# A gated two-layer block on one core: expert matmuls in FP32 without splits, sixteen feed-forward panels loaded during routing, eleven from the 37th expert block on

## The reference

```python
x = x + tanh(g_xattn[0]) * cross_attention(layernorm(x), ctx)       # 64 context rows per sequence
x = x + tanh(g_ffn[0])   * moe(layernorm(x))                        # see below
x = x + tanh(g_xattn[1]) * (layernorm(x) @ W1.T + mean(ctx) @ W2.T + b)
x = x + tanh(g_ffn[1])   * ternary_ffn(layernorm(x))                # 256 -> 1024 -> 1024 -> 1024 -> 256

def moe(x):   # 16 experts, hidden width 128, two experts per token
    scores = softmax(x @ gate_w); w, idx = top_k(scores, 2); w = w / sum(w)
    h = silu(x @ w1[e]) * (x @ w3[e]);  y = h @ w2[e]               # for both chosen experts e
    return sum(w * y) + x
```

## Time and profile before

| | |
|---|---|
| median of the runs | 514.05 us |
| runs | 511.73 to 516.06 us (3) |
| the profiled execution | 516.89 us, span 514.8 us |
| TensorE busy | 482.9 us (94%) |
| VectorE, ScalarE, Pool busy | 317.2, 214.0, 147.2 us |
| mean granted TensorE clock | 0.973 |
| moved by transfers | 58.81 MB |

### The profile page before, as it was taken

How to read it: one execution, slowest core, us unless ns; L and a number is a source line. 1 busy time by engine, 2 the same in 40 slices (tenths; PEclk the granted TensorE clock), 3 DMA queues, 4 the chain that set the end, 5 groups by cost and what they waited for, 6 DMA issues and landing times.

```text
span 514.8 us, 7849 instructions
## 1 busy us (share of the span) xinstructions
PE 482.9 (94%) x2754; PEld 414.0 (80%) x2754; DVE 317.2 (62%) x850; ACT 214.0 (42%) x444; POOL 147.2 (29%) x154
## 2 busy tenths in 40 slices
PE   8898977994889899999999999999999999999996
PEld 7787867893879678888987888897888888788886
DVE  3988855872668577548456874537677633745433
ACT  4569924671547695621254221126222133621210
POOL 1677674647562141101071110126011101000000
PEclk9989997997799999999999999999999999999999
DMA  8967432795572558422041220005032002021101
GB/s 290 339 251 245 156 93 83 211 290 167 166 220 94 177 185 268 148 81 61 22 143 43 64 78 24 1 1 163 22 102 62 1 1 81 2 77 66 42 1 47
DMA packets 34480, 58.81 MB, mean 114 GB/s; under 512 B 4545, under 2 KB 18369, under 8 KB 34370
## 3 DMA queue, kind: packets, MB, share of 16 engines
q1 hardware_dynamic: 29776, 47.12, 27.9%
q0 software_dynamic: 3840, 10.49, 7.2%
q10 hardware_dynamic: 818, 0.61, 0.4%
HBM read 47.85 MB, written 14.42 MB: 121 GB/s over the span
## 4 chain that ended last, share of the span: by engine, by line
PE 77%; DVE 4%; another core or an unknown queue 3%; ACT 2%; issue 2%; DMA 1%; POOLq 0%
PE bank L2038 23%; PE bank L2039 23%; PE bank L2010 6%; PE bank L2007 5%; PE bank L1613 3%; PE bank L1615 3%; PE bank L1614 3%; PE bank L2071 3%; PE bank L2070 3%; PE bank L1850 2%; PE bank L1853 1%; DVE turned L1019 1%; ACT xb L1429 1%; DMA xg_more<-xb_dram,perm 1%
## 5 line engine op out<-in xcount | busy, mean ns | idle before, releaser
L1587 ACT ACTIVATE sg<-bank,colv 128x512 f32<-128x512 f32 x64 | 44.1, 690 | 177.2 <-PE bank L2039 177.2
L2038 PE MATMUL bank<-Ah,Wr 128*128 128x512 f32 x256 | 100.3, 392 | 0.6 <-DVE sg L1296 0.6
L2038 PE MATMUL bank<-Bh,Wr 128*128 128x512 f32 x256 | 99.9, 390 | 0.0
L2039 PE MATMUL bank<-Bl,Wr 128*128 128x512 f32 x256 | 99.7, 389 | 0.0
L2039 PE MATMUL bank<-Al,Wr 128*128 128x512 f32 x256 | 99.7, 389 | 0.0
L2038 PEld LDWEIGHTS bank<-Ah,Wr 128*128 128x128 f32 x256 | 48.0, 188 | 11.9 <-DVE sg L1296 1.4
L2039 PEld LDWEIGHTS bank<-Bl,Wr 128*128 128x128 f32 x256 | 48.1, 188 | 9.8
L2038 PEld LDWEIGHTS bank<-Bh,Wr 128*128 128x128 f32 x256 | 48.1, 188 | 9.8
L2039 PEld LDWEIGHTS bank<-Al,Wr 128*128 128x128 f32 x256 | 48.1, 188 | 9.7
L1313 DVE CAST Ah<-sg 128x512 fp32r<-128x512 f32 x32 | 13.6, 426 | 60.1 <-ACT sg L1587 60.1
L1613 PE MATMUL bank<-EL,turned 128*128 (+1 forms) x133 | 42.7, 321 | 1.2 <-issue 0.9
(11 more groups left out here) (295 smaller groups left out, 1036.9 us busy)
## 6 DMA issues: line engine op xcount, KB each, us to landing
Wraw<-panels SPq DMA_DIRECT2D x44, 256.0 KB
stage<-panels SPq DMA_DIRECT2D x44, 256.0 KB
ES<-experts SPq DMA_DIRECT2D x16, 384.0 KB, 5.7
ys_dram<-yb SPq DMA_DIRECT2D x47, 128.0 KB
ys_dram<-x SPq DMA_DIRECT2D x1, 1920.0 KB, 8.8
X<-x SPq DMA_DIRECT2D x3, 512.0 KB, 7.8
xb_dram<-xb SPq DMA_DIRECT2D x3, 512.0 KB, 4.5
out<-outb SPq DMA_DIRECT2D x3, 512.0 KB
```

The costliest lines, as they stand in the source:

```text
L1587: eng.activation(sg[:, (8 * layer + m) % 3, :], bank[m % 4][:, :], ACT.Gelu, scale=colv[:, c + m:c + m + 1]).then_inc(f_act[m], 1)
L2038: mm(bank[m % 4][:, :], Wr[:, base:base + P], h[0][:, k, :], start=k == 0, stop=False)
L2039: ins = mm(bank[m % 4][:, :], Wr[:, base:base + P], h[1][:, k, :], start=False, stop=k == FK - 1 and not general)
```

## The change

- The experts are no longer split. All sixteen are loaded unsplit to `EW` (FP32), with no wait, over `Ah`, `Al`, `Bh`. `split_high`, `split_low`, `expert_low` and the buffers `ES` go.
- Gate, up and down are one FP32 matmul each per 128 of depth: three per block for nine. `turned` is FP32, in four buffers, copied by ScalarE alone (`rows_turned`); `low` goes. The first `gate_up` waits for all experts.
- The top sixteen panels of `Wr` are now free during routing. A new function `home` puts panels 0 to 15 there; SP loads eight behind the first group's `store_rows` and eight behind the second's. Panels 16 to 26 are loaded at blocks 36 to 46, one each, and 27 to 43 when the loop is over (those from 38 on after the first layer).
- Fill transfers stand behind experts 7, 13 and 15; all `store_rows` behind the experts.
- Eight gather buffers for six, two product buffers for three, `down` three blocks later instead of four, the permutation after block 1 instead of 2, the comparisons for it (`block_hot`) ahead of the loop. The y gathers go two at a time at blocks 32 to 35; the written-out numbers of the first group's steps move by about one.

```diff
-PAN_AT = 8
-
-FILL_AT = (10, 11)
-DVE_LOW_AT = (5, 7, 9, 11)
-
-PERM_AT = 2
-FIRST_PAN = NRAW + (3 * 4 * 4 * 256) // (4 * 512)
+PAN_AT, PAN_BETWEEN = 36, 11
+
+FILL_FIRST, FILL_AT = 7, (13, 15)
+
+PERM_AT = 1
+FIRST_PAN = 2 * NRAW + (3 * 4 * 4 * 256) // (4 * 512)
...
-Y_AT = (28, 29, 31, 32, 34, 35, 37, 38)
-ROOT2_AT, ROW_AT, ROOT3_AT = (37, 45), (38, 45), (44, 46)
-ADD_AT, STAT_AT = (25, 28, 31, 36), (26, 29, 33, 37)
-TURN3_AT, HIGH3_AT, LOW3_AT, PART_AT, X3_AT = (30, 37), (31, 38), (32, 39), (33, 40), (34, 41)
+Y_AT = (32, 32, 33, 33, 34, 34, 35, 35)
+ROOT2_AT, ROW_AT, ROOT3_AT = (38, 45), (39, 45), (44, 46)
+ADD_AT, STAT_AT = (27, 29, 32, 35), (28, 30, 33, 36)
+TURN3_AT, HIGH3_AT, LOW3_AT, PART_AT, X3_AT = (31, 38), (32, 39), (33, 40), (34, 41), (35, 42)
 NORM_AT, TURN4_AT, HIGH4_AT, LOW4_AT = (43, 45), (44, 47), (45, 48), (46, 48)
...
-NXG = 6
-DOWN = 4
+NXG = 8
+DOWN = 3
...
-        put = over(e_off, b_end)
-        EH, EL = put("EH", [P, E * EXP_COLS], F32R), put("EL", [P, E * EXP_COLS], F32R)
+        put = over(w_end, bl_off)
+        EW = put("EW", [P, E * EXP_COLS])
+        put = over(bl_off, b_end)
+        XT = 4
+        turned = [put(f"turned{b}", [P, JW]) for b in range(XT)]
+        xg_late = put("xg_late", [P, NXG - 6, D])
...
+        def home(w):
+
+            return (w + NPAN - NRAW) % NPAN * PANEL
...
-            eng.dma_start(Wraw[:, w * PANEL:(w + 1) * PANEL], panels[w]).then_inc(dma_pan[w % 4], 16)
+            eng.dma_start(Wraw[:, home(w):home(w) + PANEL], panels[w]).then_inc(dma_pan[w % 4], 16)
...
             def load_expert(e):
-                if e >= NES:
-
-                    eng.wait_ge(pool_el, EL_CUT * (e - NES + 1))
-                eng.dma_start(ES[:, e % NES, :], experts[e]).then_inc(dma_exp[e % NES], 16)
+                eng.dma_start(EW[:, e * EXP_COLS:(e + 1) * EXP_COLS], experts[e]).then_inc(dma_exp[e % 2], 16)
...
-            for e in range(NES, E):
+            for e in range(E):
                 load_expert(e)
-                if e == NES + 1:
+                if e == FILL_FIRST:
 
                     eng.dma_start(ys_dram[T * TOPK:NBLK * P, :], x[0:NBLK * P - T * TOPK, :]).then_inc(dma_fill, 16)
                 if e in FILL_AT:
                     n = T * TOPK - E * P
                     a, b = (n * (FILL_AT.index(e) + k) // len(FILL_AT) for k in range(2))
                     eng.dma_start(ys_dram[E * P + a:E * P + b, :], x[a:b, :]).then_inc(dma_fill, 16)
-                if e == 12:
-                    store_rows(0, 0, TG)
-            store_rows(1, 0, TG)
-
-            store_rows(2, 0, TG)
+            for g in range(NG - 1):
+                store_rows(g, 0, TG)
+                if g < 2:
+                    for w in range(NRAW // 2 * g, NRAW // 2 * (g + 1)):
+                        load_raw(eng, w)
             eng.wait_ge(dve_xb, 2)
             eng.dma_start(xb_tiles[:, NT - 2:NT, :], xb[:, 1, 2:TG, :]).then_inc(dma_xb[1], 16)
             store_rows(NG - 1, 0, 2)
...
-            panel_at = [PAN_AT + 3 * (w // 2) + w % 2 if w < DVE_PAN else PAN_AT + 12 + 2 * (w - DVE_PAN) for w in range(NRAW)]
+            panel_at = [PAN_AT + n for n in range(PAN_BETWEEN)]
...
-            split_low(2)
-            factor1(1)
-            split_low(2)
-            eng.wait_ge(dve_pn, 1)
-            factor1(2)
-            split_low(2)
-            factor1(3)
-            split_low(2)
+            for g in range(1, NG):
+                factor1(g)
             for g in range(NG):
-                if g > 0:
-                    eng.wait_ge(dve_ohr, g)
-                    split_low(2)
-                if g < NG - 1:
-                    eng.wait_ge(dve_pn, g + 2)
-                else:
-                    eng.wait_ge(dve_both, NG)
-                split_low(3 if g < NG - 1 else 1)
                 factors2(g)
...
-                if i in Y_AT:
-                    gather_rows(0, [Y_AT.index(i)])
+                gather_rows(0, [n for n in range(TOPK * TG) if Y_AT[n] == i])
...
-                if i < 2:
-                    block_hot(i)
-                if i <= PERM_AT:
+                if i < NBLK:
                     product(i)
-                    if i == PERM_AT:
-                        experts_of_blocks()
-                        eng.wait_ge(pe_perm, 2)
-                        permuted(bank_y[0], slice(E, NBLK))
-                    low(i + 2)
-                else:
-                    low(i + 2)
-                    if i < NBLK:
-                        product(i)
-
+                if i == PERM_AT:
+                    experts_of_blocks()
+                    eng.wait_ge(pe_perm, 2)
+                    permuted(bank_y[0], slice(E, NBLK))
                 if i == PERM_AT + 1:
                     block_experts()
-                if i in DVE_LOW_AT:
...
-            def high_turned(n):
-                b, w = n % 3, joint(n)
+
+
+            def rows_turned(n):
                 eng.wait_ge(b_tx, n + 1)
-                eng.activation(turned_pair(n)[0][:, w], bank_t[b][:, w], ACT.Copy).then_inc(b_xh, 1)
+                eng.activation(turned[n % XT][:, joint(n)], bank_t[n % 3][:, joint(n)], ACT.Copy).then_inc(b_xt, 1)
...
             def gate_up(i, at_):
-                high_, low_ = turned_pair(i)
-                eng.wait_ge(b_xl, i + 1)
+                eng.wait_ge(b_xt, i + 1)
+                if i == 0:
+                    eng.wait_ge(dve_counts, 1)
+                    for b in range(2):
+                        eng.wait_ge(dma_exp[b], 16 * (E // 2))
                 if i >= 2:
 
                     eng.wait_ge(b_h, i - 1)
                 for k in range(DK):
-                    w = bass.ds(at_ + k * 2 * H, 2 * H)
-                    x_k = slice(k * P, (k + 1) * P)
-                    ins = three(bank_gu[i % 2][:, 0:2 * H], (high_[:, x_k], low_[:, x_k]), (EH[:, w], EL[:, w]),
-                                k == 0, k == DK - 1)
+                    ins = mm(bank_gu[i % 2][:, 0:2 * H], turned[i % XT][:, k * P:(k + 1) * P],
+                             EW[:, bass.ds(at_ + k * 2 * H, 2 * H)], start=k == 0, stop=k == DK - 1)
                 ins.then_inc(b_gu, 1)
 
             def down(i, at_):
-                eng.wait_ge(b_xl, i + 5)
+                eng.wait_ge(b_xt, i + 5)
                 if i == 0:
 
                     eng.wait_ge(dve_perm, 2)
                 elif i >= 2:
                     eng.wait_ge(b_ye, i - 1)
-                w = bass.ds(at_ + 2 * DK * H, D)
-                h = (i + 4) % 3
-                three(bank_y[i % 2][:, 0:D], (t_high[h][:, DK * P:JW], t_low[h][:, DK * P:JW]), (EH[:, w], EL[:, w]),
-                      True, True).then_inc(b_y, 1)
+                mm(bank_y[i % 2][:, 0:D], turned[i % XT][:, DK * P:JW], EW[:, bass.ds(at_ + 2 * DK * H, D)], start=True,
+                   stop=True).then_inc(b_y, 1)
 
 
             offsets = [e * EXP_COLS for e in range(E)]
```

## The result

The changed kernel took 517.73 us (median of six runs, 517.11 to 522.37) beside 512.2 us for the kernel before in the same runs: a ratio of 1.0112, with an interval of 1.0074 to 1.015. I had predicted 504.5 with a range of 496 to 514. It became slower by about 5.5 us where I expected it to become faster by 9.5.

A forecast was written before the change was run, and what follows sets the result against it. TensorE's matmul chain was taken to bound the block loop at 1.40 us a block, with 32 us of waits or lower clock besides. +10 - 18 - 0.5 - 2 + 1 = -9.5 us gave 504.5 for the median, range 496 to 514.

The forecast's parts named there:

- Matmuls in FP32: Expert blocks: three FP32 matmuls for nine FP32R make a block 1.62 us against 1.40, +10 us if TensorE stays the bound.
- The remainder: Block stage: the 32 us in which TensorE waited or ran at the lower level fall to 14, -18 us.
- Eight buffers and the new place of the sums' gathers: Block loop, sums' gathers at blocks 32 to 35: a TensorE wait of about 1 to 3 us replaces 15.
- Panels: Routing: sixteen panels moved there fit only just, last stores following at 61 to 62; +1 us (0 to +5).
- Splits: Routing: without Pool's expert splits, VectorE's small instructions beside them no longer stretch; -2 us (bounds 0 and -4).
- The stalls stay: Block stage, rival: stalls come with Pool's unbroken gather bursts, so about 32 us stay; +7.5, 521.5 us, chance 0.12.
- less than 5 of the 32 us go: Block stage: the point from which the slow rival, 521.5 us, was to be decided; its chance 0.12.

The follow-up runs named there:

- fp32r_nine: Changed kernel with nine FP32R matmuls per block again, on high parts, instead of three FP32: 514.29 us with stalls, 493.13 without.
- y_old: Changed kernel with the sums' gathers at the block numbers of before (28 to 38) instead of 32 to 35: 519.07 us, ratio 1.0106, with stalls.
- loop_panels: Changed kernel with its first sixteen panels loaded at blocks 4 to 19, one each, instead of in routing: 493.33 us, ratio 0.9948, without stalls.
- splits_back: `loop_panels` with 24 subtractions of Pool put back into routing where the expert splits were, on a scratch tile: 515.82 us, ratio 1.0059, with stalls.
- after_again: Changed kernel, unchanged, run and profiled again beside the kernel before: 518.55 us, ratio 1.0087, with stalls.

## Why the prediction was wrong, point by point

- **Matmuls in FP32.** The step was right: 1.62 us by six records, +10.3 in the floor. What followed, "+10 if TensorE stays the bound", was not what it was worth. Without stalls B stayed at 86.7 for 86.8, and by `fp32r_nine` the longer step is worth 3.5 to 4.3 us of time.
- **The remainder, 32 to 14, -18 us.** This is the step that failed. With stalls it went from 32.1 and 29.1 (two profiles of before) to 23.7 and 25.4, by about 6; without, from 14.5 to 4.1, by 10.4. I had put it down to rows that land late because Pool is behind. That mechanism exists, and the sets without stalls show it (5.3 us of waits for landings in B before, none after); but in the sets with stalls, from which the profile came, it was not the main one. There TensorE's results reached ScalarE late while Pool issued gathers without a pause, and the change left such rows of gathers in place. The sign was in the rows that I read: ScalarE waited 4.53 us for the result that it took at 130.14, and no wait of TensorE behind 119.72 named a landing. By the count of records that result was complete at 118.29, 11.9 us earlier. I charged the whole stall to the 1.08 us wait for a landing at 119.72.
- **Eight buffers and the new place of the sums' gathers.** The place is worth nothing with stalls (`y_old`). Whether the buffers or the longer step closed the 10.4 us without them was not taken apart beyond this: with nine FP32R matmuls and eight buffers the remainder is 83.2 - 72.3 = 10.9, so 3.6 of the 10.4 come without the longer step and the other 6.8 with it.
- **Panels, +1 us (0 to +5).** Wrong in size: F to T grew from 7.2 to 11.6, 13.8 and 12.3 us, so +4.4 to +6.6; `loop_panels` gives all of it back. I forecast the last landing at 61 to 62, and Pool's first gather came at 61.7, 62.7 and 64.2. I compared that with the 65.21 of a profile in which routing happened to end late, and did not ask what the earlier end of VectorE's chain would be worth if the stores did not follow it. The store's longer way (+2.9) and TensorE's lower clock after the wait (+1.4) are what my +1 left out.
- **Splits, -2 us in routing.** Too small, by profiles: the factors are ready at 54.5 to 54.8 in three of the changed kernel and at 57.20, 60.83 and 62.72 in three of before, so the gain is 2.6 to 8 us. The casts take 0.17 us four times, as forecast. Putting Pool's part back cost about 1 us, so most of the gain belongs to something else that the change did to routing (ScalarE's splits, the loads of the experts that no longer wait); this was not taken apart.
- **The sum** by measured terms, with stalls, all from the means of two profiles each: factors 54.5 for 59.0, -4.5; F to T 12.7 for 7.2, +5.5; B 107.1 for 102.9, +4.2; together +5.2. Measured: +5.5 and +4.6 (518.55 against 513.94). Without stalls there is one profile of each: F to T +5.1, B -0.1, and factors 54.75 for 62.72; but the profiled execution of before was 4.7 us above the median of its set, so the last term is worth less than the 8.0 that it shows. Measured: +1.1 (497.18 for 496.1).
- **The rivals.** "The stalls stay" named what happened: unbroken gathers, a remainder that hardly falls, a result slower than before, with +7.5 for the measured +5.5. I gave it 0.12. Its decisive point ("less than 5 of the 32 us go") was missed narrowly, at about 6. Against it I had written that TensorE waits for a landing at 119.72; that was the wrong row to weigh.

A version that beats both kernels without stalls is `loop_panels` (0.993 to 0.995). With stalls it was not run; `splits_back`, the same with Pool's work added, is at 1.0059 there, below the changed kernel's 1.0087 in the same set.

## What to carry to other kernels

When a consumer gets its data microseconds after the producer's last record and no landing is named, do not explain the gap by the nearest late transfer: replace the suspected neighbours by work of the same length that moves nothing. When a step frees an engine ahead of a store, look at what stands before that store on its queue, and at the clock of the engine that waits for it: here panels and rows ahead of the last store took back most of what routing had gained. And read a stage's length from more than one profile before counting microseconds in it: the last factors of the same kernel came at 57.2, 60.8 and 62.7.

## What was unexpected of the hardware

The same program lost 15 to 21 us of its block stage in stalls in some sets of runs and none in others (before: B of 101.4 and 104.4 against 86.8; changed: 106.3 and 108.0 against 86.7), all runs of a set alike. In the stalls ScalarE took TensorE's results up to 9.7 us after their last record in the changed kernel and 11.9 in the kernel before (0.04 undisturbed). TensorE's own idle time in the second stall ended 0.06 us after VectorE's product or 0.15 after ScalarE's copy, so the signals the other way came as promptly as ever; in the first stall it also stood up to 1.9 us (until 78.37 in `after_again`) where nothing that it could have waited for had just ended. Delays of more than 2.1 us came only in or just behind rows of gathers about 1.25 us apart, and in the second stall they went where gathers were replaced by computing. What differs between the sets is open. So is the path by which Pool's gathers reach TensorE's.
